# A fused adaLN block on one core: mask and weight loads, masking and turning moved ahead of modulation sums 2 and 3

## The reference

```
mod = (silu(c) @ wmod)            # wmod 1024 x 6144, six rows of 1024
sa, ca, ga, sb, cb, gb = mod
h = layernorm(x) * (1 + ca) + sa  # x: 2048 tokens x 1024
x = x + ga * (h @ (weight * block_on).T + bias)
...
```

## Time and profile before

| | us |
|---|---|
| median of 3 executions | 1124.25 |
| lowest, highest | 1122.67, 1124.4 |
| the profiled execution's own time | 1126.06 |
| its span, first to last instruction | 1124.3 |
| TensorE busy | 1089.5 (97%) |
| VectorE busy | 739.7 (66%) |
| ScalarE busy | 428.7 (38%) |
| POOL busy | 375.0 (33%) |

### The profile page before, as it was taken

One profiled execution on the slowest core, in us unless ns is written; L12 is line 12 of the kernel. 1 busy time (PEld: TensorE's weight loads), 2 busy tenths in 40 slices (PEclk: granted clock), 3 DMA queues, 4 the chain that ended last, 5 costly groups with the idle time before them and its releaser, 6 DMA issues. The chain is left out here.

```text
span 1124.3 us, 13245 instructions
## 1 busy us (share of the span) xinstructions
PE 1089.5 (97%) x4741; PEld 509.9 (45%) x4741; DVE 739.7 (66%) x926; ACT 428.7 (38%) x783; POOL 375.0 (33%) x346
## 2 busy tenths in 40 slices
PE   4899999999999999999999999999999899999998
PEld 1544454555444444444444444444444344444444
DVE  2739367767678898888797888879545343334434
ACT  1332236656556455445555555555432000000000
POOL 1105237546655353315655564655200000000000
PEclk8699999999999999999999999999999999999999
DMA  9993212426353555446666665675288665565431
GB/s 342 404 387 83 75 40 73 113 57 203 125 197 103 166 173 177 116 126 195 183 206 192 188 180 175 194 198 178 76 345 333 235 245 230 218 245 220 184 144 38
DMA packets 130001, 206.94 MB, mean 184 GB/s; under 512 B 20624, under 2 KB 99216, under 8 KB 127504
## 3 DMA queue, kind: packets, MB, share of 16 engines
q1 hardware_dynamic: 124640, 184.08, 49.8%
q0 software_dynamic: 5296, 22.02, 5.5%
HBM read 137.39 MB, written 68.68 MB: 183 GB/s over the span
## 5 line engine op out<-in xcount | busy, mean ns | idle before, releaser
L1302 PE MATMUL pA<-work 128*128 128x512 f16 x1680 | 377.0, 379 | 4.6 <-ACT work L1043 2.9
L1302 PEld LDWEIGHTS pA<-work 128*128 128x128 f16 x1680 | 163.7, 98 | 205.1 <-ACT work L1043 6.0
L1166 PE MATMUL pA<-work 128*128 128x512 f32 x512 | 225.0, 593 | 0.0
L1302 PE MATMUL pB<-work 128*128 128x512 f16 x752 | 175.9, 379 | 1.4 <-DVE work L1700 1.4
L1166 PEld LDWEIGHTS pA<-work 128*128 128x128 f32 x512 | 95.0, 190 | 112.3 <-issue 111.4
L1722 DVE SCALAR_TENSOR_TENSOR work<-work 128x512 f16<-128x512 f16 x144 | 122.8, 875 | 19.2 <-ACT work L1063 19.0
L1369 PE MATMUL pA<-work 128*128 128x512 f16 x600 | 134.4, 379 | 0.0
L913 ACT ACTIVATE work<-pB,small 128x128 f32<-128x128 f32 x256 | 92.6, 477 | 72.2 <-PE pB L1155 60.9
L1043 ACT ACTIVATE work<-pA 128x512 f32<-128x512 f32 x126 | 74.6, 592 | 116.4 <-PE pA L1302 111.2
L1302 PEld LDWEIGHTS pB<-work 128*128 128x128 f16 x752 | 73.5, 98 | 90.1 <-DVE work L1700 2.1
L1369 PE MATMUL pB<-work 128*128 128x512 f16 x480 | 109.0, 383 | 3.3 <-DMA work<-h_left_scratch 3.3
(11 more groups left out here) (170 smaller groups left out, 1067.7 us busy)
## 6 DMA issues: line engine op xcount, KB each, us to landing
work<-h_scratch SPq DMA_DIRECT2D x8, 4480.0 KB, 13.7
h_scratch<-work SPq DMA_DIRECT2D x60, 512.0 KB, 3.1
work<-in_L_wmod SPq DMA_DIRECT2D x10, 2048.0 KB, 16.2
work<-in_L_ffn_gate_w SPq DMA_DIRECT2D x84, 128.0 KB, 3.3
work<-in_L_ffn_up_w SPq DMA_DIRECT2D x84, 128.0 KB, 2.9
work<-down_scratch SPq DMA_DIRECT2D x7, 1280.0 KB, 11.5
work<-in_L_ffn_down_w SPq DMA_DIRECT2D x68, 128.0 KB, 2.8
work<-in_L_attn_data SPq DMA_DIRECT2D x16, 512.0 KB, 4.4
```

The lines of the kernel that those rows point to most:

```text
L1166: last = pe.matmul(pA[:, 2 * par(t) + h, :], hT1[par(t)][:, c, :], wT[:, c, h * H:(h + 1) * H], start=(c == 0), stop=(c == KT - 1))
L1302: last = pe.matmul(ps, w[:, m, c], bc[b][:, mv_, s, c], start=begin, stop=(i == n - 1 and c == KT // 2 - 1 and s == 1), skip_group_check=True)
```

## The change

It moves loads and the work on them, and adds none.

- SP: masks 0 to 3 go between token tile 0 and piece 0, the first four weight tiles between pieces 1 and 2, token tile 1 behind piece 3. The second masks and weights and all that follows keep their order.
- TensorE: row sum 0, mask total 0, row sum 1, columns 0, turns 0 to 3, row sum 2, row sum 3, columns 1, transpose(0,1), and then the first attention as before.
- VectorE: the first masking and the first four moves go ahead of token tile 1's normalisation.
- POOL: the first mask multiply goes ahead of the statistics and the copy of token tile 1.
- ScalarE: the four moves of the first turns go between the copies of rows 1 and 2, and so ahead of turn_out(0).
- PSUM: row sums 2 and 3 go to pB 2 and pA 1, and the columns to the upper half of pB 3. Two waits are new on TensorE: for the mask bits ahead of columns 0, and for three of ScalarE's moves ahead of row sum 3.

```diff
-        colp = pB[:, 2, 0:2 * KT]
+        colp = pB[:, 3, H // 2:H // 2 + 2 * KT]
...
-        rowsum = [pA[:, k, :] for k in range(4)] + [pB[:, 2 + k % 2, :] for k in range(6)]
+        rowsum = [pA[:, 0, :], pA[:, 1, :], pB[:, 2, :], pA[:, 1, :]] + [pB[:, 2 + k % 2, :] for k in range(6)]
...
             load_x(0)
+            load_masks(0)
             load_piece(0)
             load_piece(1)
-            load_x(1)
+            load_weights(0)
             load_piece(2)
             load_piece(3)
-            for g in range(2):
-                for r in range(4 * g, 4 * g + 4):
-                    sp.dma_start(mst[r], m_v[r]).then_inc(m_loaded[r], 16)
-                for r in TURNS[4 * g:4 * g + 4]:
-                    sp.dma_start(wst[r], w_v[r]).then_inc(w_loaded[r], 16)
+            load_x(1)
+            load_masks(1)
+            load_weights(1)
             load_piece(4)
...
             rstd_of(0, 0)
             pool.tensor_copy(xg[0], xt[0]).then_inc(x_copied, 1)
-            rstd_of(0, 1)
-            pool.tensor_copy(xg[1], xt[1]).then_inc(x_copied, 1)
-
             for n in range(2, KT, 4):
                 pool.wait_ge(mask_bits, n // 4 + 1)
                 pool.wait_ge(w_loaded[TURNS[n]], 16)
                 mask_rows(pool, TURNS[n], masked_by_pool)
+                if n == 2:
+                    rstd_of(0, 1)
+                    pool.tensor_copy(xg[1], xt[1]).then_inc(x_copied, 1)
...
-            for m in range(4):
-                copy_row(m)
+            def move_row_half(u):
+                act.wait_ge(w_turned, u + 1)
+                act.activation(*move_rows(u), ACT.Copy).then_inc(wT_ready, 1)
+
+            copy_row(0)
+            copy_row(1)
+            for u in range(4, KT):
+                move_row_half(u)
+            copy_row(2)
+            copy_row(3)
...
             turn_out(0)
-            def move_row_half(u):
-                act.wait_ge(w_turned, u + 1)
-                act.activation(*move_rows(u), ACT.Copy).then_inc(wT_ready, 1)
-
-            for u in range(4, KT):
-                move_row_half(u)
             turn_out(1)
...
-            for m in range(4):
-                row_sum(m)
-                if m % 2:
-                    columns(m // 2, colp[:, KT * (m // 2):KT * (m // 2 + 1)])
+            row_sum(0)
             mask_total_of(0)
+            row_sum(1)
+            pe.wait_ge(mask_bits, 1)
+            columns(0, colp[:, 0:KT])
             for n in range(4):
                 turn_rows(n)
+            row_sum(2)
+            pe.wait_ge(wT_ready, 3)
+            row_sum(3)
+            columns(1, colp[:, KT:2 * KT])
             transpose(0, 1)
...
             norm1(0)
-            norm1(1)
             mask_rows_of(0)
             for u in range(4):
                 dve.wait_ge(w_turned, u + 1)
                 dve.tensor_copy(*move_rows(u)).then_inc(wT_by_dve, 1)
+            norm1(1)
             mask_rows_of(1)
```

More of the change, by code:

```diff
@@ L574, in _, with load_masks, load_weights @@
             sp.dma_start(cvec, c_in.rearrange("o (p t) -> (o p) t", p=P)).then_inc(c_loaded, 16)
+            def load_masks(g):
+                for r in range(4 * g, 4 * g + 4):
+                    sp.dma_start(mst[r], m_v[r]).then_inc(m_loaded[r], 16)
+            def load_weights(g):
+                for r in TURNS[4 * g:4 * g + 4]:
+                    sp.dma_start(wst[r], w_v[r]).then_inc(w_loaded[r], 16)
             load_x(0)
+            load_masks(0)
             load_piece(0)
             load_piece(1)
-            load_x(1)
+            load_weights(0)
             load_piece(2)
             load_piece(3)
-            for g in range(2):
-                for r in range(4 * g, 4 * g + 4):
-                    sp.dma_start(mst[r], m_v[r]).then_inc(m_loaded[r], 16)
-                for r in TURNS[4 * g:4 * g + 4]:
-                    sp.dma_start(wst[r], w_v[r]).then_inc(w_loaded[r], 16)
+            load_x(1)
+            load_masks(1)
+            load_weights(1)
             load_piece(4)
```

## The result

The changed kernel takes 1129.64 us (median of five, 1128.08 to 1131.28) against 1124.25 us before (1122.67 to 1124.67): ratio 1.0053, 95% interval 1.0038 to 1.0068, so 5.4 us slower by the medians. The forecast was 1127.0 us, 2.75 us slower: the sign was right, the size half of what came. The profiled execution took 1129.03 us, its span is 1127.2 us.

The account below looks back on a forecast made before the run. TensorE was taken as the bound, so only the start of its gapless full-clock work counts. 1.25 + 1.5 = +2.75 us made 1126.06 into 1128.8 us profiled, 1127.0 us median; range 1123.3 to 1130.0 us.

Parts of the forecast that it names:

- Landings: Load stream of the head: piece 3 lands at 39.2 us; second masks, weights and piece 4 land as before.
- Turns leave the path: First turns on TensorE: end between 35.1 and 38.3 us, and leave the path to the first attention entirely.
- rival C: Head: turns never raise the clock and hold up row sums 2 and 3; +5.45 us, 1129.7 us; chance 0.13.
- What takes their place: Ahead of first attention: row sum 3, copy, columns, tile 0's shift and scale come last; attention at 50.5 us, +1.25 us.
- Token tile 1 ... transposed by 46.6 us, ahead of 50.5: nothing: Head: token tile 1 is normalised at 44.6 us and transposed before the first attention, so it costs nothing.
- The clock behind it: First attention: low-clock time there costs between 0 and 3.05 us; the middle, +1.5 us, was taken.
- Rival B: Head: the clock, raised in the turns, is never lost; -2.2 to -2.8 us, 1121.5 to 1122.0 us; chance 0.09.
- That execution is 1.8 us above the median ... so the predicted median is 1127.0 us: Whole kernel: 1128.8 us for the profiled execution, put 1.8 us lower for the median.
- I therefore take the change of the time as the shift of that first attention, plus what a low clock costs behind it: Whole kernel: later waits move along with the first attention, so only its shift and low-clock cost count: +2.75 us.
- The two rules of the Trainium skill: TensorE clock: avoiding long gaps prevents drops (sum -2.2 us); transposes don't count as activity (sum +5.45 us).

Follow-up runs that it names:

- the second trace: The changed kernel run again with no edit, for a second trace and more executions: 1129.99 us.
- fillers: Added 128x512 matmuls, results unused, in the head's gaps: seven in the changed kernel, 1122.24 us; nine in the kernel before, 1121.52 us.
- the control at the start: The kernel before with seven small matmuls, results unused, ahead of the first transpose: 1120.19 us.
- the seven at the start: Seven small 128x128 matmuls, results unused, added ahead of the first transpose: changed kernel 1126.31 us, kernel before 1120.19 us.

## Why the prediction was right in sign and wrong in size

*Landings.* Right where it counts. Piece 3 was to be there at 39.2 us and was at 38.87; pieces 0 and 1 came 1.2 us early, at 16.48 and 21.79 (forecast 17.7 and 23.0); tile 1 at 40.0 (40.6). The second masks, weights and piece 4 made nothing wait.

*Turns leave the path.* Right, and earlier than thought: over at 31.8 us instead of 35.1 to 38.3, since the clock rose at 21.3 us, behind the mask total, and row sum 1 and columns 0 took 1.92 us each. In the second trace, where it was low until 32.1 us, they were over at 32.9 us. The 2.7 us of late row sum 3 (rival C) did not come.

*"What takes their place", +1.25 us.* Right in mechanism. The chain from piece 3 to the end of L928 took 48.09 - 38.87 = 9.2 us instead of 11.16, as row sum 3 was partly and columns 1 wholly at the high clock. By itself that would have put the attention at 48.2 us. The forecast had 0.50 in the columns and the attention released by the shift and scale; the columns ran at 1.00, and what released it was the transpose.

*"Token tile 1 ... transposed by 46.6 us, ahead of 50.5: nothing".* Wrong, and the one wait of the change that was overlooked. `transpose(0, 1)` waits for `hT1_ready`, because L928 reads tile 0 from the banks that the transpose writes. In before that was met long ago (40.81 us in the earlier trace rows, transpose at 47.98 us); with L928 moved to 48.09 us the transpose stands behind it in series, 1.73 us to the attention at 49.96. The profiled pair hid the error, since it and the lucky columns nearly cancel: forecast 50.5, measured 49.96. Taken away, it moved the attention by 2.0 us and the head by 0.5 us.

*"The clock behind it", +1.5 us.* Right: 1.0, 1.6 and 1.2 us in the three traces (first six records against 2.74 us). What before's order has there is 8 us of turns and transposes right ahead of the attention; in its five traces without fillers in the head (the control at the start is the fifth) the clock was back at 41.6 to 48.8 us, always ahead of the attention at 46.2 to 49.3 us. The changed order has 1-column matmuls and 3.4 us of idle there, and each of its traces without fillers in the head is at 0.50 from about 46 us or earlier until 52 us or later. So what the change costs here is this: it moves the dense work away from the place where it raised the clock. Rival B, faster, needed a clock that is never lost; with fillers it comes to within 0.6 us of before's order, not ahead of it.

With these terms the head is 3.0 us later on average, near the forecast's 2.75 us, but partly by luck: the overlooked 1.73 us stand against columns at the high clock.

*"That execution is 1.8 us above the median ... so the predicted median is 1127.0 us".* This is the step that failed in the sum. On the profiled execution the forecast was 1128.8 us and 1129.03 was measured; from there to the median it took 1.8 us off, and the changed kernel's median is 0.6 us above its profiled execution. These 2.4 us are nearly all of the 2.6 us that the forecast was short. The step assumed that the changed kernel shares what made that execution of before slow. Part of that was in the head: 70.24 us against 68.7 us on average in before's other three. The changed order's three heads lie within 0.4 us of each other, so none of them has such a part to lose; its three profiled executions are all below their medians, by 0.6, 3.9 and 2.9 us.

*"I therefore take the change of the time as the shift of that first attention, plus what a low clock costs behind it".* This put the stretch between the head and the feed-forward part at nothing. It was 1.64 us in the profiled pair, which is why +2.75 us came near the +2.97 measured there: luck, as the head alone made 1.73. On average it was 1.2 us, 4.2 us instead of 3.0 at the first feed-forward product, because the low stretch behind columns 3 and 4 comes in every trace of the changed order and in a third of before's. Read after the fact, it goes with where the head stands: it is in all eight traces with the columns in one row and the head up to 68.39 us, in none of the four from 68.72 to 70.24 us, and in all seven from 71.47 us on. No run tested this.

From 4.2 us to the 5.4 of the medians a part stays open. The profiled executions of the changed kernel (1129.03, 1126.07, 1126.56 us) lie below their medians, and none with a mean clock of 0.988 was traced.

*The two rules of the Trainium skill* ("TensorE: Matmul & The Clock Gate"). That it is enough to leave no long gap between bursts ("Why this matters for your kernels"): the clock fell at 45.18 us although TensorE had been idle only for 0.71 us, and for 0.3 us right ahead of the fall, since 38.87 us, and at 151 us with no gap at all, both times behind 1-column matmuls. The trace disagrees. That transposes do not count as activity ("Part 4: PE-mode transpose"): in the changed kernel's second trace it rose at 32.1 us, inside an unbroken row of turns from 27.59 to 32.9 us. The trace disagrees here too.

## What to carry to other kernels

Before moving work ahead in a list, ask what its place was worth to TensorE's clock: here the clock was up behind dense work just ahead of the critical stage in every trace, and, without fillers, low behind a chain through another engine and a row of 1-column matmuls in its place. For every step that becomes last, list the waits on its output buffers as well as on its inputs; a wait that was met long ago can become the path. A forecast for a median wants more than one trace, of both kernels, since the good and bad executions of one need not be those of the other; and an experiment that adds instructions wants a control that adds them where they do nothing.

## What was not expected of the hardware

- The granted clock turned at other moments in each execution of the same kernel (48.8 us and 41.6 us in two traces of before). The first attention was 3.1 us apart, of which 0.6 us may be later landings.
- 3.6 to 4.2 us of 1-column matmuls without a gap (token tile 5) were followed by a stretch at 0.50 in 15 of the 19 traces in which they stood back to back; the one trace with them spread has none.
- With three or more added matmuls ahead of it in TensorE's list, the load near 875 us (192 KB, right behind one of 4480 KB) took 13.4 to 14.5 us instead of 15.1 to 16.1; with the seven at the start the time was lower by 3 to 4 us for both kernels. Behind the load they did nothing. The cause is open.
